# A graph network kernel: the middle stage moved into the last hop round, and node stages that find their operands ready

## The reference

```
h = relu(layernorm(x));  x = x + L0(h)      # L0: tanh, 5 APPNP hops, GIN, GIN, mish
    appnp: h = 0.8 * norm_i * segment_sum((h * norm_o)[src], dst) + 0.2 * x0
    gin:   ((1 + eps) * h + segment_sum(h[src], dst)) @ W + b;   mish(y) = y * tanh(softplus(y))
h = relu(layernorm(x));  x = x + L1(h, edge_attr)
    mlp(u) = g * layernorm(silu(silu(u @ W1 + b1) @ W2 + b2)) + beta
    twice: edges_new = mlp([h[dst], h[src], edges]) + edges;  agg = segment_sum(edges_new, dst)
           h = mlp([h, agg]) + h;  edges = edges_new
h = relu(layernorm(x));  x = x + segment_sum(w_e * (h @ W.T + b)[src], dst)
h = relu(layernorm(x));  x = x + elu(segment_sum(typed_linear(h[src], etype), dst) + h @ W_res + b_res)
```

## Time and profile before

| | us |
|---|---|
| median of the runs | 4255.19 |
| profiled execution, its own time | 4260.01 |
| its span, first to last instruction | 4257.9 |
| last round of `hops`, first to last product | about 1587 to 1688 |
| `gnn_input` (`mid_`) and its seams | about 1690 to 1799 |
| edge pass `la_` | about 1799 to 2380 |
| `node_update`, first | about 2380 to 2473 |
| edge pass `lb_` | about 2473 to 3047 |
| `node_update`, second | about 3047 to 3161 |
| two gather passes | 3161 to the end |

### The profile page before, as it was taken

How to read it: one execution, slowest core, us unless ns; L and a number is a source line. 1 busy time by engine, 2 the same in 40 slices (tenths; PEclk the granted TensorE clock), 3 DMA queues, 4 the chain that set the end, 5 groups by cost and what they waited for, 6 DMA issues and landing times. The chain is left out here.

```text
span 4257.9 us, 76630 instructions
## 1 busy us (share of the span) xinstructions
PE 3084.3 (72%) x18633; PEld 2181.0 (51%) x18633; DVE 2570.6 (60%) x9518; ACT 1354.4 (32%) x2970; POOL 2086.2 (49%) x2123
## 2 busy tenths in 40 slices
PE   2388885669999998389999669999655445644444
PEld 2266663226666665267777447777433333433333
DVE  7688886996555462768888657777653333422223
ACT  0067885950111100245555335555330000200000
POOL 0477773000000000377777257777527777267776
PEclk8578997999999999599999789999865555755555
DMA  2112222000000001366666254444411111322212
GB/s 60 42 51 68 74 75 96 2 1 30 16 16 16 17 15 34 106 176 181 182 177 172 52 143 128 130 129 127 76 45 53 53 53 53 119 73 53 53 53 55
DMA packets 247907, 325.62 MB, mean 76 GB/s; under 512 B 77964, under 2 KB 159451, under 8 KB 246523
## 3 DMA queue, kind: packets, MB, share of 16 engines
q1 hardware_dynamic: 180922, 207.94, 15.9%
q0 software_dynamic: 66656, 113.74, 11.5%
HBM read 229.22 MB, written 92.26 MB: 76 GB/s over the span
## 5 line engine op out<-in xcount | busy, mean ns | idle before, releaser
L2557 PE MATMUL gat_acc<-gat_rows,gat_hot 128*128 x1664 | 485.9, 453 | 504.6 <-SPq L2524 302.7
L1008 PE MATMUL hop_p_a<-hop_h,adj 128*128 128x384 bf16 x4375 | 712.5, 327 | 0.0
L2557 PEld LDWEIGHTS gat_acc<-gat_rows,gat_hot 128*128 128x128 f32 x1664 | 380.5, 318 | 611.3 <-issue 609.3
L1008 PEld LDWEIGHTS hop_p_a<-hop_h,adj 128*128 (+1 forms) x4375 | 427.7, 98 | 284.4 <-issue 1.5
L1952 POOL DMA_INDIRECT lb_far<-far_rows,lb_idx x416 | 407.7, 980 | 197.1 <-issue 117.9
L1952 POOL DMA_INDIRECT la_far<-far_rows,la_idx x416 | 409.5, 984 | 154.3 <-issue 117.3
L2535 POOL DMA_INDIRECT gat_rows<-typed_rows,gat_idx x391 | 372.7, 953 | 203.0 <-DVE gat_idx L2565 84.2
L2535 POOL DMA_INDIRECT gat_rows<-hidden_rows,gat_idx x391 | 371.4, 950 | 190.8 <-DVE gat_idx L2565 72.0
L1668 POOL DMA_INDIRECT by_src_records<-scatter_rec,scatter_rank x375 | 378.1, 1008 | 133.9 <-issue 100.0
L2573 DVE TENSOR_SCALAR gat_hot<-iota_row,gat_tabs 128x128 f32<-128x128 f32 x416 | 149.8, 366 | 336.8 <-PE gat_acc L2557 322.2
L560 POOL DMA_INDIRECT mid_by_src_tab_rec<-by_src_records,by_src_off x4 | 4.0, 1002 | 708.6 <-POOLq L84 707.7
(11 more groups left out here) (521 smaller groups left out, 6417.1 us busy)
## 6 DMA issues: line engine op xcount, KB each, us to landing
edge_features<-emb_out SPq DMA_DIRECT2D x104, 256.0 KB
la_feat<-edge_features SPq DMA_DIRECT2D x104, 256.0 KB
edge_features<-la_out SPq DMA_DIRECT2D x104, 256.0 KB
lb_feat<-edge_features SPq DMA_DIRECT2D x104, 256.0 KB
la_place<-dst_row SPq DMA_DIRECT2D x104, 128.0 KB
lb_place<-dst_row SPq DMA_DIRECT2D x104, 128.0 KB
typed_rows<-gat_typed_row SPq DMA_DIRECT2D x25, 512.0 KB, 2.6
cells_tabs<-x0share_nodes SPq DMA_DIRECT2D x125, 64.0 KB, 1.8
```

Of the source, the lines that this page charges most:

```text
L1008: ins = nc.tensor.matmul(p_a[(u.par + r) % 2][:, 0:3 * D], K.adj[:, s, bass.ds(u.t * P, P)], h3[r % 2][:, s, :, :].rearrange("p i d -> p ( ...
L2557: nc.tensor.matmul(acc[:, bass.ds(tile[u % LOADS], D)], hot[u % HOTS][:, :], rows[:, bass.ds(row[u % LOADS], D)], start=False, stop=True, ...
```

## The change

The stage `gnn_input` is gone. Its work on nodes is done inside the last round of `hops`, in pairs of tiles (`PAIRS`, 12 pairs and a single one), one or more tiles behind the products: DVE (`clipped`, `mish`, `measured`, `rooted`, `split_near`, `low`), POOL (two elementwise operations and one power for each pair), ACT (`exp`, `norm`, `new_T`, `high`, `middle`) and PE (`turned`, `weighed`). The round's loop is written out. The inverse root is now a power of -1/2 on POOL, a TENSOR_TENSOR of 2 or 4 columns, in place of the Newton steps. x and h go to memory (`x_nodes`, `h_nodes`), and the edge pass loads them with agg. `NodeWeights` holds the weights of the node stage; SP loads them at group 24 of the edge pass. From group 40 on DVE makes `b2r` and, every fourth group, `base` there. In the node stage DVE makes `gathered` two quads ahead, and POOL only the powers. The `by_src` tables are built in the first node stage, with one PSUM bank for the three of them. The diff, cut to its core:

```diff
-        banks = [ph.ps(f"{lay.name}_tab_p_t{i}", [P, 4, P]) for i in range(n_tab * NB)]
+        banks = [ph.ps(f"{lay.name}_tab_p_t{i}", [P, 4, P]) for i in range(1 if shared else n_tab * NB)] * (n_tab if shared else 1)
...
+            if shared and i >= 1:
+                pe.wait_ge(s_out, i)
...
+    PAIRS = [list(range(t, min(t + 2, NT))) for t in range(0, NT, 2)]
...
+            def turned(q):
+                pe.wait_ge(s_ln, q + 1)
+                if q >= 1:
+                    pe.wait_ge(s_hT, q)
+                for k in range(width(q)):
+                    ins = nc.tensor.transpose(p_h[:, k * P:(k + 1) * P], hh[q % 2][:, k, :], K.ident[:, :])
+                ins.then_inc(s_hTp, 1)
+            def weighed(q):
+                pe.wait_ge(s_hT, q + 1)
+                if q >= 2:
+                    pe.wait_ge(s_out, q - 1)
+                    pe.wait_ge(s_rest, q - 1)
+                for k in range(width(q)):
+                    ins = nc.tensor.matmul(p_o[q % 2][:, k, :], hT[q % 2][:, k, :], w, start=True, stop=True)
+                ins.then_inc(s_o, 1)
+            pe.wait_ge(s_w, 48)
+            for t in range(NT + 5):
+                if t < NT:
+                    pe.wait_ge(s_a2, NT + t - 1)
+                    products(Turn(t, t % 2, t // 2, t < 2), HOPS + 1)
+                q = t // 2 - 2
+                if t % 2 == 0 and live(q):
+                    turned(q)
+                if t % 2 == 1 and live(q):
+                    weighed(q)
...
+            for t in range(2 * NP + 5):
+                q = t // 2
+                if t % 2 == 0:
+                    if live(q - 2):
+                        norm(q - 2)
+                    if live(q - 3):
+                        high(q - 3)
+                    if q == NP - 1:
+                        exp(q)
...
+            for q in range(NP):
+                c = width(q)
+                pool.wait_ge(s_num, q + 1)
+                nc.gpsimd.tensor_tensor(o[q % 2][:, 0:c, :], o[q % 2][:, 0:c, :], num[:, 0:c, :], ALU.mult).then_inc(s_on, 1)
+                pool.wait_ge(s_mish, q + 1)
+                pool.wait_ge(*x_sem(q))
+                nc.gpsimd.tensor_tensor(x_of(q), x_of(q), o[q % 2][:, 0:c, :], ALU.add).then_inc(s_x, 1)
+                pool.wait_ge(s_v, q + 1)
+                if q >= 2:
+                    pool.wait_ge(s_ln, q - 1)
+                nc.gpsimd.tensor_tensor(rstd[q % 2][:, 0:c], v[:, 0:c], K.neghalf[:, 0:c], ALU.pow).then_inc(s_root, 1)
...
+            def gin2(t):
+                q, k, r = t // 2, t % 2, HOPS + 1
+                g = got[(t + r) % 2]
+                dve.wait_ge(s_sum, r * NT + t + 1)
+                nc.vector.scalar_tensor_tensor(
+                    g[:, :, :].rearrange("p i d -> p (i d)"), h3[r % 2][:, t, :, :].rearrange("p i d -> p (i d)"),
+                    K.eps[:, 1:2], p_a[(t + r) % 2][:, 0:3 * D], ALU.mult, ALU.add).then_inc(s_a2, 1)
+                dve.wait_ge(s_a2, NT + t + 1)
+                ch3(nc.vector.tensor_tensor(g[:, 1, :], g[:, 1, :], g[:, 2, :], ALU.add))
+                if k == 0 and q >= 2:
+                    dve.wait_ge(s_x, q - 1)
+                nc.vector.tensor_tensor(o[q % 2][:, k, :], g[:, 1, :], g[:, 0, :], ALU.add).then_inc(s_z, 1)
...
+            def clipped(q):
+                c = width(q)
+                dve.wait_ge(s_z, PAIRS[q][-1] + 1)
+                ch3(nc.vector.tensor_tensor(o[q % 2][:, 0:c, :], o[q % 2][:, 0:c, :], across(b2, q), ALU.add))
+                if q >= 1:
+                    dve.wait_ge(s_num, q)
+                nc.vector.tensor_scalar(e[:, 0:c, :], o[q % 2][:, 0:c, :], 20.0, None, ALU.min).then_inc(s_clip, 1)
...
+            def mish(q):
+                c = width(q)
+                dve.wait_ge(s_e, q + 1)
+                if q >= 1:
+                    dve.wait_ge(s_on, q)
+                nc.vector.scalar_tensor_tensor(num[:, 0:c, :], e[:, 0:c, :], 2.0, e[:, 0:c, :], ALU.add, ALU.mult)\
+                    .then_inc(s_num, 1)
...
+                for k in range(c):
+                    nc.vector.bn_stats(stats[:, k, :], x_of(q)[:, k, :]).then_inc(s_stats, 1)
+                dve.wait_ge(s_stats, PAIRS[q][-1] + 1)
+                if q >= 1:
+                    dve.wait_ge(s_rstd, q)
+                for k in range(c):
+                    nc.vector.bn_aggr(mv[:, k, :], stats[:, k, :]).then_inc(s_mv, 1)
+                dve.wait_ge(s_mv, PAIRS[q][-1] + 1)
+                nc.vector.tensor_scalar(v[:, 0:c], col(1, c), LN_EPS, None, ALU.add).then_inc(s_v, 1)
...
+            for t in range(NT):
+                gin2(t)
+                q = t // 2
+                if t % 2 == 1:
+                    if live(q - 1):
+                        measured(q - 1)
+                    clipped(q)
+                    if live(q - 1):
+                        rooted(q - 1)
+                else:
+                    if live(q - 3):
+                        split_near(q - 3)
+                    if live(q - 1):
+                        mish(q - 1)
+                    if t == NT - 1:
+                        clipped(q)
+                    if live(q - 3):
+                        low(q - 3)
+            measured(NP - 2)
+            rooted(NP - 2)
+            mish(NP - 1)
+            measured(NP - 1)
+            rooted(NP - 1)
+            for q in range(NP - 3, NP):
+                split_near(q)
+                low(q)
...
-def gnn_input(nc, A, K, dr):
...
+                if g == 24:
+                    W.load(sp, s_node_w)
...
+                if keeps and 1 <= g <= 3 * NB:
+                    t, q = (K.agg, K.h, K.x)[(g - 1) // NB], (g - 1) % NB
+                    lo, hi = QUADS[q][0], QUADS[q][-1] + 1
+                    sp.dma_start(t[:, lo:hi, :].rearrange("p t d -> p (t d)"),
+                                 (dr.agg, dr.hn, dr.xn)[(g - 1) // NB][:, lo * D:hi * D]).then_inc(s_node if g > NB else s_agg, 16)
...
+            def base(q):
+                quad = lambda t: t[:, QUADS[q][0]:QUADS[q][-1] + 1, :]
+                n = len(QUADS[q])
+                ins = nc.vector.tensor_tensor(quad(W.base), quad(K.h), W.beta_row[:, :].unsqueeze(1).to_broadcast([P, n, D]),
+                                              ALU.add)
+                if not keeps:
+                    ch(ins)
+                    ins = nc.vector.tensor_tensor(quad(W.base), quad(W.base), quad(K.x), ALU.add)
+                ins.then_inc(s_base, 1)
...
+                if g == BASE:
+                    dve.wait_ge(s_node_w, W.loads * 16)
+                    if keeps:
+                        dve.wait_ge(s_node, 2 * NB * 16)
+                    bias_parts(nc, ch, K, W.b2r, W.b2x3, W.b2h, W.b2p).then_inc(s_base, 1)
+                if BASE < g <= BASE + 4 * NB and g % 4 == 0:
+                    base((g - BASE) // 4 - 1)
...
+class NodeWeights:
...
+    def load(self, sp, sem):
+        A = self.A
+        W1, b1, W2, b2, g, beta = (A["L1_gnn_" + v][self.layer] for v in ("nW1", "nb1", "nW2", "nb2", "ng", "nbeta"))
+        broadcast_row(sp, self.ge_row[:, :], A["L1_gnn_eg"][self.layer], sem)
...
-                if q > 0:
-                    cp(nc.gpsimd.tensor_tensor(nodes(K.sum, q), nodes(K.sum, q), wide(ge_row, q), ALU.mult))
-                    cp(nc.gpsimd.tensor_tensor(nodes(K.agg, q), nodes(K.agg, q), nodes(K.sum, q), ALU.add))
-                    pool.sem_inc(s_agg, 1)
-                else:
-                    pool.wait_ge(s_w, LOADS * 16)
-                    pool.wait_ge(s_agg, 1)
-                ins = nc.gpsimd.tensor_tensor(nodes(K.sum, q), nodes(K.h, q), wide(beta_row, q), ALU.add)
+                c = width(q)
+                pool.wait_ge(s_v, q + 1)
+                if q >= 2:
+                    pool.wait_ge(s_n, q - 1)
+                nc.gpsimd.tensor_tensor(rstd[q % 2][:, 0:c], v[:, 0:c], K.neghalf[:, 0:c], ALU.pow).then_inc(s_pow, 1)
                 if last:
-                    cp(ins)
-                    ins = nc.gpsimd.tensor_tensor(nodes(K.sum, q), nodes(K.sum, q), nodes(K.x, q), ALU.add)
-                ins.then_inc(s_base, 1)
+                    pool.wait_ge(s_xv, q + 1)
+                    if q >= 2:
+                        pool.wait_ge(s_ln, q - 1)
+                    nc.gpsimd.tensor_tensor(xrstd[q % 2][:, 0:c], xv[:, 0:c], K.neghalf[:, 0:c], ALU.pow).then_inc(s_xpow, 1)
...
+                if not last and r in (3, 5, 7):
+                    table.tensor(pe, (r - 3) // 2)
...
+            def gathered(q):
+                ch(nc.vector.tensor_tensor(nodes(K.sum, q), nodes(K.sum, q), wide(W.ge_row, q), ALU.mult))
+                nc.vector.tensor_tensor(nodes(K.agg, q), nodes(K.agg, q), nodes(K.sum, q), ALU.add).then_inc(s_agg, 1)
...
+            gathered(0)
+            if last:
+                dve.wait_ge(s_wt, 1)
+                nc.vector.tensor_copy(wn[:, :], p_o[0][:, 0, :]).then_inc(s_wtc, 1)
+            gathered(1)
...
+                if live(r - 1):
+                    q = r - 1
```

(30 more changed lines are left out.)

614 lines of the change are left out of this document (251 added, 363 removed).

## The result

The changed kernel takes 4137.34 us (median of 4 runs, 4132.76 to 4141.19) against 4255.75 us: 118.4 us less, ratio 0.9725 (95% interval 0.9709 to 0.974). Its profiled execution has a span of 4136.7 us, 121.2 less than the one before. I forecast -107 (4148, range 4115 to 4200).

The account below looks back on a forecast made before the run. TensorE's products bound the last round, a chain of short steps the middle stage, GpSimd paces the edge passes. -68 - 14 - 29 + 4 = -107 from 4260 gives 4153, less 4.8 is 4148 us; range 4115 to 4200.

Parts of the forecast that it names:

- Last round: Last hop round, with the middle stage's work added: about 119 us in place of 101.8, +17.
- Tail: After the last round's products: 20 us to the last store; round plus tail 139 against 207.6 us, -68.
- The power: Inverse root on GpSimd in round and node stages: cost proportional to columns, 0.45 us for 2, 0.8 for 4.
- First node stage: Stage after the first edge pass: earlier eviction, no bias wait, shorter moments to norm; -14 with steady part and tables.
- steady -4 and table +6: First node stage after its start: steady quads gain 4 us, `by_src` table work in gaps adds 6.
- Second node stage: Stage after the second edge pass: eviction -11.7, bias wait -4.6, moments to norm -8.6, steady part -4; together -29.
- Edge passes: Both edge passes: added VectorE adds, bias parts and loads, mostly absorbed; +4 us, 20 if nothing hid them.
- Port: Rival, round, tail and node stages: VectorE's slowing beside GpSimd is complete, not partial; 4168 us, chance 0.12.
- Dear power: Rival, round and node stages: each power has a fixed price, 2.2 us; 4184 us, chance 0.14 (full price 0.05).
- Better clock: Rival, node stages: denser work gives TensorE full clock, about 20 us go; 4125 us, chance 0.12.
- Slower: Rival, edge passes: added VectorE work starves TensorE and its clock halves; 30 groups give 4304 us, chance 0.04.
- a round of 200 us: Rival, last round not covered: TensorE waits 4 us a tile, the 68 are lost; 4216 us, chance 0.03.

Follow-up runs that it names:

- the repeats: The kernel before and the changed kernel, each run again unaltered on one experiment chip: 5228.2 and 5116.8 us.
- bias_late: Changed kernel, but the bias parts are made in the node stage again, after the second weighted sum: 5076.1 us, ratio 0.9776 to the kernel before.
- nodes_newton: Changed kernel, but VectorE makes both node stages' inverse roots with three Newton steps, not GpSimd's power: 5100.0 us, ratio 0.9825 to the kernel before.
- weights_late: Changed kernel, but weights are loaded and bias parts and base made in the node stage again: 5149.6 us, ratio 0.983 to the kernel before.

## Why the prediction was right

- **Last round, +17 forecast, +11.3 measured.** The mechanism was right, and so were the durations of TensorE and VectorE. What was mis-sized is the stall: I gave VectorE 0.65 us a pair of delay beside GpSimd and TensorE up to 0.5 us a pair of waiting. No VectorE operation of a full pair was delayed, its work came to 7.7 us a pair and not 9.1, which left 1.5 us of slack, and TensorE waited 0.3 us in the whole round. A pair costs 1.08 us over its products, not 1.5.
- **Tail, -85 forecast, -87.1 measured.** Last product to last store is 20.3 us, forecast 20. The seam shrank from 4.6 to 3.2 us, which I had called unchanged.
- **The power.** 0.81 and 1.01 us in place of 0.45 and 0.8: the fixed part that I set at 0.1 us is about 0.4 by the four sizes, and the rival of a dear power (2.2) was nearer in kind than in size. It did not matter in the round, where VectorE waits 0.27 us for it, and its worth against Newton on an otherwise unchanged kernel is shown: 18.6 us in the round and tail, 20.9 in the second node stage, nothing clear of the spread in the first.
- **First node stage, -14 forecast, -12.8 measured** (-8.3 by the repeats, and this stage varies by 5 us). The start gave 16.4 (forecast 15.8), and the rest of the sum, steady -4 and table +6, came to +3.6 (forecast +2). The number of the start was right because what I added up were measured waits, and the change removed them all. Two of its three causes were wrong. The eviction came 4.0 us sooner (forecast 4.4); that is the weights. From there to the moments 6.4 us went, which I put down to bias parts that stand in the way (5.3), and from the moments to the norm 6.0, which I put down to Newton's steps (6.1). Both were GpSimd holding up VectorE's small operations. bias_late puts the parts back and loses nothing, and in nodes_newton, with Newton back, the moments are 3.9 us from the norm, not 8.9: the power is worth 1.0 of the 6.0 us.
- **Second node stage, -29 forecast, -31.6 measured.** Start -26.0 (forecast -25), the rest -5.6 (forecast -4). In the start the eviction came 12.1 us sooner (forecast 11.7, to the same instant); the moments were 11.4 us from the norm before, 3.9 in nodes_newton and 2.9 with the power, so the power is worth 1.0 of the 8.6 us forecast for it.
- **Edge passes, +4 forecast, +3.9 measured**, and by the repeats +1.2 for both. weights_late shows no cost of weights, bias parts and base there. What the 4.3 us of the first trace are stays open.
- **Rivals.** Port: a real effect with a narrower condition than the rival had. In the round's steady part it costs only GpSimd, 0.11 us an operation, and the powers, which the rival charged with 10 us, hold nothing up. I weighed it on the middle stage alone, where six of seven rows met nothing, and overlooked the start of the node stages, where it cost the kernel before more than 10 us each time. Dear power: not at 2.2 us. Better clock: the node stages' clock rose from 0.72 and 0.67 to 0.79 and 0.74; the forecast priced no such rise, and no run parts its share from the rest. Slower: edge passes keep their length.
- **Slips in the rivals' sums.** Port sets VectorE's 10.6 us against a pair of 9.9, where the forecast's own pair is 9.6; that adds 3 us to its 4168. With a round of 200 us in place of 119 the case comes to about 4229, not 4216. Full clock takes 4148 to 4128, not 4125. None changes the forecast.
- **What is left.** Of the 14 us between 107 and the traces' 121.2, 9 lie in the stages above and 4.9 in stages that didn't change.

## What to carry to other kernels

A stage of short dependent steps costs little inside a stage that one engine fills, if each other engine keeps slack in every turn: here 1.1 us a pair of TensorE's own time, 11.3 us in all, bought back 87 us. A wait is named after what came last in the trace, not after what made it late: look at how long the operations behind it take elsewhere in the same trace (1.26 against 0.28 us here), and undo one cause at a time before two of them are counted. And work with no deadline (a table) put in one block in front of an in-order engine's urgent work holds up all that waits for that engine; cut to the size of its waits it gave 12.7 us in one stage.

## What the hardware showed

- GpSimd and VectorE: a VectorE operation with two SBUF inputs or a single-input fp32 one between SBUF tiles that starts during a GpSimd addition or multiplication of two tiles waits for its end (0.86 for 0.42, 0.65 for 0.23, and on 3 partitions 1.26 for 0.28 us); a reciprocal, and an operation with one input in PSUM, don't. Started 0.04 to 0.16 us earlier it keeps its time and GpSimd's takes 0.83 or 0.84 for 0.72. The power delays none that began during it.
- The power on GpSimd costs 0.56, 0.81, 1.01 and 4.33 us for 1, 2, 4 and 25 columns of 128 partitions.
- The same kernel takes 4255 us in the first comparison and 5195 to 5238 on the three chips of the experiments, nearly all of it in the stages with indirect DMAs, while the hop rounds agree to the tenth (712.2). Whether it is the chip or its condition at the time, no run shows.
